# Cross-attention decoder layer: six projections moved to other key tiles, and maxima chunks spread one to four a tile

## The reference, cut to what matters

```python
# x (32, 56, 128), ctx (32, 1500, 128); 16 heads of 8
x = layernorm(x + self_attention(x))
q, k, v = heads(x @ wq), heads(ctx @ wk), heads(ctx @ wv)
scores  = einsum('bhtd,bhsd->bhts', q, k) + relative_bias      # (32, 16, 56, 1500)
weights = softmax(scores, axis=-1)
x = layernorm(x + (einsum('bhts,bhsd->bhtd', weights, v)) @ wo)
x = layernorm(x + ffn(x))            # 128 -> 512 -> 512 -> 512 -> 128
```

## Time and profile before

| | us |
|---|---|
| median of 3 runs | 977.25 |
| the profiled execution, its own time | 974.32 |
| its span | 972.5 |
| TensorE busy | 920.7 (95%) |
| VectorE busy | 721.1 (74%) |
| ScalarE busy | 607.7 (62%) |
| POOL busy | 354.0 (36%) |

### The profile page before, as it was taken

How to read it: one execution, slowest core, us unless ns; L and a number is a source line. 1 busy time by engine, 2 the same in 40 slices (tenths; PEclk the granted TensorE clock), 3 DMA queues, 4 the chain that set the end, 5 groups by cost and what they waited for, 6 DMA issues and landing times.

```text
span 972.5 us, 26041 instructions
## 1 busy us (share of the span) xinstructions
PE 920.7 (95%) x10410; PEld 645.6 (66%) x10410; DVE 721.1 (74%) x1705; ACT 607.7 (62%) x1359; POOL 354.0 (36%) x317
## 2 busy tenths in 40 slices
PE   6777799999999999999999999999999998999996
PEld 3554477777777777777777777777777777555564
DVE  5657778888888888888888888888888995600023
ACT  2322477777777777777777777777777666622232
POOL 8200545554444445545555444445544200000000
PEclk9866999999999999999999999999999999999999
DMA  8738677666667777776666667777676503000001
GB/s 211 260 82 169 164 223 214 187 199 183 183 202 213 197 201 205 197 207 199 192 200 183 184 189 210 200 206 206 194 201 190 152 3 123 1 1 0 1 10 28
DMA packets 56324, 154.96 MB, mean 159 GB/s; under 512 B 23234, under 2 KB 35322, under 8 KB 53114
## 3 DMA queue, kind: packets, MB, share of 16 engines
q1 hardware_dynamic: 55820, 152.44, 55.2%
q10 hardware_dynamic: 384, 0.86, 0.3%
HBM read 110.03 MB, written 42.63 MB: 157 GB/s over the span
## 4 chain that ended last, share of the span: by engine, by line
PE 56%; DVE 30%; issue 2%; DMA 1%; ACT 1%; SPq 1%; DVEq 0%; ACTq 0%
PE ps L113 12%; DVE near_out L120 12%; PE ps L604 10%; PE ps L897 10%; PE ps L867 9%; PE ps L944 5%; DVE rec L1012 3%; PE ps L949 3%; DVE ps L978 3%; DVE cmax L123 3%; PE ps L906 3%; DVE rec L1014 2%; PE ps L598 2%; DVE xh L1019 1%; DVE rec L990 1%
## 5 line engine op out<-in xcount | busy, mean ns | idle before, releaser
L1077 ACT ACTIVATE e_sb<-ps 128x448 f32<-128x448 f32 (+1 forms) x768 | 380.5, 560 | 143.0 <-PE ps L867 95.0
L123 DVE TENSOR_REDUCE cmax<-ps 112x1 f32<-112x512 f32 x512 | 328.1, 682 | 82.4 <-PE ps L113 82.4
L113 PE MATMUL ps<-kst,qst 111*112 111x512 bf16 (+1 forms) x768 | 265.4, 390 | 8.2 <-PEq L132 2.8
L867 PEld LDWEIGHTS ps<-qst,kst 114*128 114x128 bf16 (+1 forms) x3072 | 190.3, 100 | 90.4 <-issue 47.5
L867 PE MATMUL ps<-qst,kst 114*128 114x112 bf16 (+1 forms) x3072 | 223.5, 213 | 4.7 <-ACT e_sb L1077 4.5
L120 DVE CUSTOM_DVE_ANT_0 near_out<-ps,near_nat 112x476 bf16<-112x476 f32 x256 | 154.5, 632 | 4.2 <-PE ps L113 4.2
L897 PE MATMUL ps<-e_sb,vals 128*32 128x168 f32 (+1 forms) x3072 | 149.4, 312 | 0.0
L1143 POOL TENSOR_TENSOR x_own<-x_sb,own 128x280 f32<-128x280 f32 x32 | 21.0, 656 | 328.3 <-ACT x_sb L1089 328.3
L1129 POOL TENSOR_TENSOR kpart<-k_left,kpart 128x500 bf16<-128x500 f32 x90 | 102.4, 1137 | 67.2 <-ACT k_left L1053 59.6
L113 PEld LDWEIGHTS ps<-kst,qst 111*112 111x112 bf16 x768 | 86.9, 130 | 55.5 <-issue 26.1
L897 PEld LDWEIGHTS ps<-e_sb,vals 128*32 128x32 f32 (+1 forms) x3072 | 80.2, 109 | 46.6 <-issue 39.6
(11 more groups left out here) (125 smaller groups left out, 916.1 us busy)
## 6 DMA issues: line engine op xcount, KB each, us to landing
kst<-kparts SPq DMA_DIRECT2D x192, 375.0 KB, 6.9
kparts<-kpart SPq DMA_DIRECT2D x90, 375.0 KB, 3.1
ctxt<-in_ctxT SPq DMA_DIRECT2D x31, 750.0 KB, 7.9
qst<-qslots SPq DMA_DIRECT2D x192, 28.0 KB, 7.2
qslots<-qst SPq DMA_DIRECT2D x4, 672.0 KB, 10.5
kparts<-kst SPq DMA_DIRECT2D x6, 375.0 KB, 3.3
qslots<-kst SPq DMA_DIRECT2D x24, 56.0 KB, 4.1
kst<-in_h SPq DMA_DIRECT2D x1, 1024.0 KB, 5.6
```

The source lines that it names most:

```text
L113: return nc.tensor.matmul(dst[0:TT, 0:hi - lo], m.qst[0:M_ROW, r, p, :], m.kst[0:M_ROW, r, p, lo:hi], start=True, stop=True)
L123: return nc.vector.tensor_reduce(m.cmax[:, r, c, p:p + 1], src[0:TT, 0:BOUND[c + 1] - BOUND[c]], AX.X, ALU.max)
L867: mm = nc.tensor.matmul(st_ps[0:K, w % ST_BANKS, p * TT:(p + 1) * TT], m.kst[0:AUG, u % RING, 4 * h + p, j * P:j * P + K], m.qst[0:AUG, u ...
L1077: nc.scalar.activation(e_sb[0:K, j % E_RING, h * HALF:(h + 1) * HALF], st_ps[0:K, w % ST_BANKS, 0:HALF], ACT.Exp).then_inc(s_ex, 1)
```

## The change

Three tables change. Counts of instructions stay the same on every engine; only their places move.

```diff
-        MISC = {8: ("v", 0, 2), NMT: ("nmt", 0, 1), 10: ("v", 1, 2), 0: ("k", 0, 3), 1: ("v", 2, 1),
-                3: ("k", 1, 3), 5: ("k", 2, 3), 7: ("den", 0, -1)}
-        LATE, AT_ONCE = (1, 3, 5), (0, 2)
+        MISC = {0: ("k", 0, 3), 2: ("v", 2, 1), 5: ("k", 1, 3), 7: ("den", 0, -1), 8: ("k", 2, 3),
+                NMT: ("nmt", 0, 1), 10: ("v", 0, 2), 11: ("v", 1, 2)}
+        LATE, AT_ONCE = (5, 10), (0, 3, 8)
+        MANY = {8: 1, 9: 1, 10: 2, 11: 2, 0: 2, 1: 1, 2: 2, 3: 1, 4: 2, 5: 4, 6: 2, 7: 4}
...
-            for i in range(2):
-                lag, n = (1, 2 * (j + ST - M0) + i) if j < M0 else (2, 2 * (j - M0) + i)
+            lag = 1 if j < M0 else 2
+            first = sum(MANY[(M0 + i) % ST] for i in range((j - M0) % ST))
+            for n in range(first, first + MANY[j]):
...
-            if (u, j) == (FIRST + 1, 2):
+            if (u, j) == (FIRST + 1, 3):
                 user = ("k", 0, 3)
```

## The result

| | median of runs, us | profiled execution, its own time | its span | typical distance of `nmt` |
|---|---|---|---|---|
| before, the runs beside it | 976.39 (974.55 to 978.44, 4 runs) | 974.32 | 972.5 | 22.47 |
| after | 966.96 (963.72 to 968.28, 4 runs) | 968.28 | 966.5 | 21.96 |

The account below looks back on a forecast made before the run. TensorE's own work was taken as 21.86 us an iteration, with 0.61 more lost to others. From 974.3, -11.6 (full iterations), +0.2 (iteration 0 to 1) and +1.4 (stack loads) gave 964.3; plus 2.9 for the median, 967.0 us, range 957 to 974.

Parts of the forecast that it names:

- What bounds: Full iterations: TensorE's own work is 21.86 us of 22.47; 0.61 us an iteration is lost to others.
- Moving one chunk out of each of steps 8 and 9: VectorE before step 11: relieved of 1.2 us, more than the 0.61 us by which it holds TensorE, all gained.
- At the last chunk of step 7 it is again 0.1 us ahead: Chunk banks in steps 5 and 7: VectorE frees them 0.1 us ahead of need, cost 0.
- The switch: TensorE, step 11: value piece joined to value products saves leaving one float32 block, 0.15 us, for a 21.7 us floor.
- Key piece in step 8: Step 8: the piece finds its bank late behind the copy of the denominators, 0.14 us lost.
- Value piece in step 10: Step 10: the piece wants its bank at 3.84 us, freed at about 3.9, 0.05 us lost.
- In step 11: Step 11: the value piece waits for the late copy of step 10's value piece, 0.18 us lost.
- Stack loads: Loads begin 1.0 us later, 0.5 us to spare; three or four of 28 iterations late, 1.4 us lost (0 to 6).
- Iteration 0 to 1: Distance from iteration 0 to 1, 21.86 us before: gets 0.2 us longer.
- The start: Start, where VectorE bounds and the last key piece comes later: taken as 0, between -1 and +1.5 us.
- the rivals: Clean hand-overs 957 (20%), four chunks on three banks 977 (8%), stacks arrive late 992 or 1033 (5%), VectorE alone bounds (1%).
- The rule by which VectorE, the fullest engine,: Whole iteration: by busy shares it could shrink to VectorE's 19.6 us, giving 900 us; the prediction argued against it.

Follow-up runs that it names:

- e9: Kernel before with the new chunk numbers only, but step 7's two extra chunks put in step 3, projections unmoved: 963.52 us, ratio 0.9874.
- e1: Kernel before with only the new numbers of chunks per step, projections and copies left where they were: 983.76 us, ratio 1.0086.
- e2: Changed kernel with two chunks in every step as before, so only projections and copies are moved: 973.4 us, ratio 0.9970.
- e10: Kernel before with only two chunks moved, one from step 9 and one from step 1, into steps 3 and 5: 968.15 us, ratio 0.9920.
- e12: Changed kernel with the denominators made in step 4 instead of 7, and one chunk of step 7 in step 4: 967.5 us, ratio 0.9903.
- e3: Changed kernel with step 10's value piece copied at the end of step 10 and no longer in step 11: 967.24 us, ratio 0.9908.
- e7: Changed kernel with a needless 426 KB store ahead of each iteration's stack loads: 972.33 us, ratio 0.9973.
- e8: Kernel before with a needless 426 KB store ahead of each iteration's stack loads: 974.71 us, ratio 1.0001.
- e5: Changed kernel with two chunks a step for the last two batches: 966.9 us, ratio 0.9930.

## Why the prediction was right, and where it was not

The total and its sign came out, and of the middle the size: 12.0 us less, where 11.6 - 1.4 = 10.2 was forecast. But the parts of it were wrong in ways that cancelled, and two terms stood at nothing that do not cost nothing.

1. **What bounds.** Shown. The 0.61 us an iteration were VectorE's: in after the chain is TensorE's alone from 504 to 532 us, and its usual distance, 21.96, is that of its iteration 0 to 1. The wait for the near bias has gone from 41.0 us to none, but that wait measures no loss: experiment 8 (e9) keeps 28.3 us of it with the chain on TensorE. The granted clock is 1.00 in both.
2. **"Moving one chunk out of each of steps 8 and 9 takes 1.2 us off it ... I take the whole 0.61 as gone."** This is the step that failed. The same chunks put into step 7 reach the maxima unreduced, and alone they made the kernel slower (e1, 22.64). I had walked the banks ("At the last chunk of step 7 it is again 0.1 us ahead"), which says that TensorE doesn't wait, and not asked what is still queued on VectorE when the turn of the maxima comes. In e9 the same relief without that queue gives 22.04. The projections, to which I gave no part of the 0.61, are worth 0.27 alone (e2): they lay key and value pieces over VectorE's busy stretch in steps 8 to 2. What VectorE still holds can be read in each run as the prediction read it before, from the usual distance less that of iteration 0 to 1: before 22.47 - 21.86 = 0.61, chunks alone 22.64 - 22.09 = 0.55, projections alone 22.20 - 22.00 = 0.20, two chunks moved (e10) 22.17 - 21.89 = 0.28, and nothing with both tables (21.96 - 21.96) or in e9 (22.04 - 22.03). So the chunks alone took 0.06 from VectorE and made TensorE's own part 0.23 longer, of which the late bank of the denominators is 0.15; the projections alone took 0.41 and cost 0.14. Each alone leaves a wait, and both together leave none; that the projections cover just the queue that the chunks bring is how I read it, from e1, e2 and after, and no run shows it by itself.
3. **The switch, "there is one such block fewer: 21.86 - 0.15 = 21.7 us is the new floor".** Wrong. A block of value products costs 0.10 to 0.20 us to leave, whatever comes next: a chunk 0.37 against 0.22, three chunks 0.79 against 0.65 (e12), scores 0.50 against 0.40, a key piece 1.04 against 0.84 (e1), a value piece 1.09 against 0.89. Projections are no continuation of that block, though both are float32. So joining them saved nothing.
4. **Key piece in step 8, 0.14 us lost.** Measured 0.99 - 0.84 = 0.15, and e9's value piece pays the same. Freeing the bank sooner does not give it back here, since the maxima then hold TensorE (e12).
5. **Value piece in step 10, 0.05.** It takes 0.89: nothing lost. **In step 11, 0.18.** The size was right, 0.20, and the cause wrong: with the copy 0.74 us early it is the same (e3). It is item 3 once more. The errors of 3 and 5 nearly cancel: 22.05 forecast, 21.96 measured. (The sum as its terms stand is 21.86 - 0.15 + 0.37 = 22.08, a gain of 0.40 and not 0.43 an iteration, 10.8 us and not 11.6.) Without any of the three terms, 21.86 + 0.15 = 22.01 would have been as good.
6. **Stack loads, 1.4 us for three or four iterations.** Three, at 0.80, 0.37 and 0.72 above 21.96, together 1.9 us. The loads begin 0.9 us later where 1.0 was forecast. That room was there before and is gone now was shown by pushing both kernels (e7, e8).
7. **Iteration 0 to 1, 0.2 longer.** 0.1.
8. **The start, 0 (-1 to 1.5).** In the profiled execution it costs 2.5 us. Part of that is landing times, I think, which isn't shown. From the first chunk to `nmt` of iteration 0 the changed order took 46.5, 45.6, 45.9, 44.7 and 44.7 us in five profiles (after, e3, e5, e7, e12) and the old one 44.0 and 44.6 in two (before, e8). The means differ by 1.2 us, and the two groups lie just apart. Kernels with one of the tables moved lie there too: 45.7 with the chunks alone, 45.8 with the projections alone, 45.7 in e9 and 45.9 in e10. So neither table has this cost to itself, and what it comes from is open.
9. **The tail** had no term. It costs 2.5 us, from both tables (2.0 with the chunks alone, 1.2 with the projections alone, and only 0.4 in e9). Without key projections the last iterations are short for TensorE, so four chunks in a step meet VectorE sooner than in the middle. Two chunks a step there give back 0.6 (e5). What the other 1.9 us are is open.

Made against the profiles, the working says 964.3, and 968.28 was measured, 4.0 more: 2.5 at the start, 2.5 in the tail and 0.9 before the first chunk, less 1.9 in the middle and from iteration 0 to 1. The forecast then added 2.9 us, because the profiled execution of before lay that much below its median, while that of after lies 1.3 above its own: 4.2 us from which executions were profiled. These two cancel. That the median of 966.96 came out at 967.0 is luck; the working earns a miss of some 4 us.

Of the rivals none came. The rule by which VectorE, the fullest engine, would let an iteration shrink to VectorE's busy time would now read 435.95 / 595 = 73% for the weight loads, 538.88 / 595 = 91% for VectorE and 538.88 / 27 = 20.0 us, with the chain on TensorE alone and the distance at 21.96: the trace does not agree with it here either.

## What to carry to other kernels

When work is moved from one step to another, ask of each queue not only whether its banks are free in time, but how much of it is unserved where the busy stretch of that engine begins. Here that is just before the maxima: with the chunks alone the burst of step 7 came back in full, and with the projections moved too TensorE had work of its own to cover it. Run each half of a two-part change alone before believing which half paid. Price the first and last iterations as well, where the work that covers a burst isn't there, and subtract what a shorter iteration takes from the time of transfers that run through it.

## What the runs showed of the hardware

- The name of a releaser is only the last event before a start. The value piece of step 11 was given as released by the copy of `vals` with 0.17 us idle before it, and with that copy 0.74 us early the gap of 0.17 us and the length of 1.16 us stayed.
- Work right behind value products (weights of 32 columns, `128*32` in the profile) takes TensorE 0.10 to 0.20 us more in the chain than the same work elsewhere: scores 0.10, one to three chunks 0.13 to 0.15, a key or value piece 0.20. I don't know what happens in it.
- Behind a wait of 2.35 us for a transfer, in iteration 0 of after, TensorE's granted clock was at the lower level. The timeline has the wait, and the windows view the 3 us behind it:

```profile
131.03 0.65 PE L113 MATMUL ps<-kst,qst 111*112 111x476 bf16 x1 [2.35 <-DMA qst<-qslots]
```

```profile
131.00:134.00 3.00, 2.97 (x12) 1.72 (x12) 0.66 (x2) 0.62 (x2) 0.00 (x0) 0.51 0.04 9
```

  The clock is 0.51 in those 3 us, so 1.2 GHz. In them the key piece takes 1.87 us, where it takes 1.11 in step 8 of the timeline above, and the scores behind it 0.94, where they take 0.56. From the start of chunk 0 to that of `nmt` it is 3.96 us, in iteration 17 2.67: 1.3 us on top of the wait. The kernel before waited 0.80 us in the same place, and e12 1.67, and their granted clock stayed 1.00; e2 waited 1.99, and it was 0.56. It is one more reason why the start differs from run to run. It can happen in the middle too. In e12 one iteration took 25.52 us instead of 22.01, with this wait and a granted clock of 0.50 over the 3 us behind it:

```profile
639.25 0.64 PE L113 MATMUL ps<-kst,qst 111*112 111x476 bf16 x1 [1.93 <-DMA qst<-qslots]
```
